# A four-layer gated transformer on one core: in layer 0, GpSimd makes the squares, cubes and sums of the spline bases in halves

## What is computed

```
out = _layernorm(res + out, ln_g, ln_b)          # res is the query projection
base = silu(out) @ base_w.T
for k in range(1, SPLINE_ORDER + 1):             # SPLINE_ORDER is 3; eight bases remain
    bases = (x - grid[:, :-(k+1)]) / (...) * bases[..., :-1] + (grid[:, k+1:] - x) / (...) * bases[..., 1:]
spl = bases.reshape(rows, -1) @ (spline_w * spline_scaler[..., None]).reshape(D, -1).T
return base + spl
```

## Time and profile before

| | us |
|---|---|
| median of 3 runs | 2756.57 |
| lowest, highest run | 2755.38, 2758.04 |
| the profiled execution | 2756.28 |
| its span, first to last instruction | 2754.5 |
| busy: PE, PEld | 2611.9, 1980.6 |
| busy: DVE, ACT, POOL | 1544.9, 1297.4, 642.9 |
| L629, GpSimd's cubes, 32 of them | 70.0 |
| L638, its sums, 32 | 66.7 |
| L624, its squares, 32 | 56.0 |

### The profile page before, as it was taken

One profiled execution on the slowest core, in us unless ns is written; L12 is line 12 of the kernel. 1 busy time (PEld: TensorE's weight loads), 2 busy tenths in 40 slices (PEclk: granted clock), 3 DMA queues, 4 the chain that ended last, 5 costly groups with the idle time before them and its releaser, 6 DMA issues. The chain is left out here.

```text
span 2754.5 us, 56714 instructions
## 1 busy us (share of the span) xinstructions
PE 2611.9 (95%) x19818; PEld 1980.6 (72%) x19818; DVE 1544.9 (56%) x4177; ACT 1297.4 (47%) x3610; POOL 642.9 (23%) x626
## 2 busy tenths in 40 slices
PE   6999978999999999989899998999998999989998
PEld 4777755666666666656677766999996777768887
DVE  4777846555555555535787874332335888842222
ACT  4777733343434334331576663333335777732222
POOL 1666661000000000000444441222221111113232
PEclk9999989999999999989999999999999999999999
DMA  4000002000000000010000005999992000059896
GB/s 124 18 18 18 12 4 107 14 13 7 13 7 13 7 13 7 1 34 1 19 20 19 24 7 210 334 327 328 329 326 76 24 19 24 7 207 311 303 313 224
DMA packets 91812, 267.57 MB, mean 97 GB/s; under 512 B 25068, under 2 KB 50805, under 8 KB 77269
## 3 DMA queue, kind: packets, MB, share of 16 engines
q1 hardware_dynamic: 74356, 242.53, 25.4%
q0 software_dynamic: 13632, 18.62, 3.2%
q10 hardware_dynamic: 3616, 3.67, 0.4%
HBM read 248.13 MB, written 16.65 MB: 96 GB/s over the span
## 5 line engine op out<-in xcount | busy, mean ns | idle before, releaser
L825 PEld LDWEIGHTS a_full_ps<-ident,a_probs 112*125 112x125 f32 x2688 | 367.7, 190 | 118.4 <-issue 57.9
L1928 PEld LDWEIGHTS m_banks<-m_x_inT,m_w 128*128 128x128 f32 x3824 | 435.1, 192 | 15.2 <-issue 13.5
L1928 PE MATMUL m_banks<-m_x_inT,m_w 128*128 128x128 f32 x3824 | 442.2, 276 | 1.4 <-ACT m_x_inT L1999 0.9
L936 ACT ACTIVATE a_probs<-a_masked,a_negmax 112x375 f32<-112x375 f32 x512 | 305.8, 599 | 283.2 <-DVE a_negmax L1155 283.1
L825 PE MATMUL a_full_ps<-ident,a_probs 112*125 112x112 f32 x2688 | 414.1, 280 | 14.3 <-DVE a_pT L1181 5.2
L1181 DVE COPY a_pT<-a_full_ps 125x448 f32<-125x448 f32 x448 | 276.6, 621 | 230.0 <-PE a_full_ps L825 226.7
L725 PE MATMUL a_full_ps<-attention_room 128*125 128x256 f32 (+1 forms) x960 | 330.1, 473 | 9.7 <-ACT a_qT L926 3.9
L717 PE MATMUL a_full_ps<-attention_room 128*128 128x375 f32 x896 | 323.0, 489 | 13.8 <-PEq L1771 8.6
L1155 DVE CUSTOM_DVE_ANT_0 a_masked<-a_sc_ps,a_mask_add 112x375 f32<-112x375 f32 x512 | 249.8, 545 | 28.5 <-PE a_sc_ps L812 27.6
L936 ACT ACTIVATE a_probs<-a_sc_ps,a_negmax 112x375 f32<-112x375 f32 x384 | 216.7, 575 | 89.6 <-DVE a_negmax L1161 89.5
L843 PEld LDWEIGHTS a_o_ps<-a_pT,a_v 125*32 125x32 f32 (+1 forms) x5376 | 164.7, 118 | 128.7 <-issue 100.3
(11 more groups left out here) (253 smaller groups left out, 3480.7 us busy)
## 6 DMA issues: line engine op xcount, KB each, us to landing
m_w<-in_L2f_w SPq DMA_DIRECT2D x105, 1024.0 KB, 6.5
m_w<-in_L3f_w SPq DMA_DIRECT2D x72, 768.0 KB, 6.1
attention_room<-in_ctxT SPq DMA_DIRECT2D x64, 375.0 KB, 3.1
m_w<-in_L3f_w SPq DMA_DIRECT2D x36, 640.0 KB
m_b<-in_L2f_b SPq DMA_DIRECT2D x35, 128.0 KB, 8.2
p_rows<-normed SPq DMA_DIRECT2D x16, 224.0 KB, 6.3
attention_room<-in_L0x_spline_wT SPq DMA_DIRECT2D x1, 2048.0 KB, 10.6
net_room<-in_L1f_w SPq DMA_DIRECT2D x2, 1024.0 KB
```

The lines of the kernel that those rows point to most:

```text
L825: mm = pe.transpose(full_ps[0:KT, bank_of["turn", i, k], (j % 4) * S:(j % 4 + 1) * S], probs[:, i % 2, a, t * KT:(t + 1) * KT], ident[0:S, ...
L936: act.activation(probs[:, i % 2, a, 0:SK], src, ACT.Exp, bias=negmax[:, m:m + 1], scale=-1.0 if mask else 1.0, accum_out=rowsum[:, par, n: ...
L1928: mm = pe.matmul(ab_ps[:, (par * FC + f) % RING, i * SLOTS:(i + 1) * SLOTS], w[:, par, c, f * P:(f + 1) * P], x_inT[:, c, :], start=(c == ...
```

## The change

Each of GpSimd's squares, cubes and sums becomes two instructions, one for bases 0 to 3 and one for bases 4 to 7, of 448 numbers in a partition each. Both halves raise the semaphore, so a batch has 12 counts in place of 6, and every wait is set to the count of the second half. Results and the order of everything else are the same. The lines behind the change move down by up to 8: `square` is L627, `cube` L634, `add_bases` L645 in the changed kernel.

```diff
@@ -258,7 +258,9 @@
 KAN_SILU, KAN_CUBE1, KAN_LATE = 2, (0, 1), 3
 KAN_TANH, KAN_ABS, KAN_ACTS_EARLY = 0, (1, 2), 3
 KAN_NEAR2, KAN_NEAR1, KAN_SQ1, KAN_ACTS_LATE = (0, 1), (2, 4), (3, 5), 6
-KAN_SQ2, KAN_CUBE2, KAN_BASES, KAN_POOLS = (0, 2), (1, 3), (4, 5), 6
+KAN_SQ2, KAN_CUBE2, KAN_BASES, KAN_POOLS = (1, 5), (3, 7), (9, 11), 12
+
+BASE_HALVES = (slice(0, 4), slice(4, 8))
 
 
 def attention_stage(core, layer, heads, hd, scale, rope=False, mask=None, kan=False, moe=None):
@@ -621,12 +623,16 @@
                 def square(b, c):
                     pool.wait_ge(s_ka2.sem, s_ka2.at(b, KAN_NEAR2[c]))
                     pool.sem_inc(s_tick[3].sem, 1)
-                    pool.tensor_tensor(sq2[:, c], near2[:, c], near2[:, c], ALU.mult).then_inc(s_kp.sem, 1)
+                    for h in BASE_HALVES:
+                        pool.tensor_tensor(sq2[:, c, h], near2[:, c, h], near2[:, c, h], ALU.mult)\
+                            .then_inc(s_kp.sem, 1)
 
                 def cube(b, c):
                     pool.wait_ge(s_kp.sem, s_kp.at(b, KAN_SQ2[c]))
                     pool.sem_inc(s_tick[3].sem, 1)
-                    pool.tensor_tensor(near2[:, c], sq2[:, c], near2[:, c], ALU.mult).then_inc(s_kp.sem, 1)
+                    for h in BASE_HALVES:
+                        pool.tensor_tensor(near2[:, c, h], sq2[:, c, h], near2[:, c, h], ALU.mult)\
+                            .then_inc(s_kp.sem, 1)
 
                 def add_bases(b, c):
                     pool.wait_ge(s_k2.sem, s_k2.at(b, KAN_CUBE1[c]))
@@ -635,7 +641,9 @@
 
                         pool.wait_ge(s_out.sem, s_out.at(b - 1))
                     pool.sem_inc(s_tick[3].sem, 1)
-                    pool.tensor_tensor(bases[:, c], near2[:, c], near1[:, c], ALU.add).then_inc(s_kp.sem, 1)
+                    for h in BASE_HALVES:
+                        pool.tensor_tensor(bases[:, c, h], near2[:, c, h], near1[:, c, h], ALU.add)\
+                            .then_inc(s_kp.sem, 1)
 
                 def kan_body(t, par):
                     if exists(t - 2):
```

## The result

| | before | changed |
|---|---|---|
| median of 8 runs each, us | 2756.31 | 2764.58 |
| lowest, highest | 2754.88, 2758.04 | 2763.24, 2767.97 |
| ratio, 95% interval | | 1.0031, 1.0022 to 1.0039 |
| span of the profiled execution | 2754.5 | 2766.1 |

The change costs 8.3 us. The forecast was 2758.2 and its range ended at 2763.1; the result lies outside it, on the side of rival C, and beyond C's own 2761.9.

The account below looks back on a forecast made before the run. TensorE's own stream was taken to set the layer-0 loop's middle turns, one batch's chain its end. Terms 1.7 - 0.5 - 0.3 + 0 + 0.7 = +1.6 us gave 2757.9, forecast as a 2758.2 median; range 2754.8 to 2763.1.

Parts of the forecast that it names:

- rival C: Middle turns: first half of the sum ends before the residual add stands in line, second goes first; 2761.9 us, chance 0.19.
- The step that failed: Middle turns: residual add waits some 0.15 us for the sum's first half, ending near 271.6, and goes ahead of the second.
- turn 2: Layer-0 loop, turn 2: residual add held for half an instruction or not at all, giving back 0.3 to 1.05; taken -0.5 us.
- turns 3 to 14: Twelve middle turns of the layer-0 loop: with no slack, 12 x 0.14 = 1.7 us slower.
- turn 15: Layer-0 loop, turn 15: normalized rows wait for half a sum, 1.1 us shorter, but TensorE waits only 0.28: -0.3 us.
- turn 16: Layer-0 loop, turn 16: one delay more and one less on VectorE, 0 us, within 0.5.
- turn 17: Last batch: nothing covers the chain of square, cube, square, cube, sum; five splits, +0.7 us (0 to 2.5).
- The price of a split: Each GpSimd split costs 0.14 us (bounds nothing to 0.51); halves 0.93 and 1.13; busy time rises 13 us.
- No slack on VectorE's path: Layer-0 loop, residual add to normalized rows: a VectorE delay of 0.35 us costs 0.35 us; slack taken as none.
- B: Rival: splits nearly free, residual add meets no sum in the middle turns, VectorE only gains; -1.0, so 2755.6 us, chance 0.14.
- D: Rival: dear splits of 0.51 us each, the sum ending 2.5 us later in middle turns; 2770 us, chance 0.05.
- E: Rival: the change does nothing to the path because the waits are for whole pairs; 2756.6 us, chance 0.12.

Follow-up runs that it names:

- the kernel with the root early: All halved as in the changed kernel, but the next stage's inverse root L188 goes ahead of the one that waits for VectorE; 2765.26 us against 2756.73 before.
- the quarters: Kernel before with only GpSimd's sums split, each into four instructions of two bases; 2767.34 us against 2756.73.
- the extra square without a wait: Kernel before, nothing halved, plus one unused GpSimd square of 448 numbers right behind the sum of chunk 1; 2774.14 us against 2756.73.
- the kernel with the late sums: Kernel before, nothing halved, with the next batch's inverse root ahead of both sums instead of between them; 2849.41 us against 2756.95.
- the pair with and without a met wait: Kernel before plus an unused square behind chunk 1's sum, waiting for chunk 0's long-done sum (ratio 1.0058) or for the sum just ahead (1.0001).

## Why the prediction was wrong, step by step

**The step that failed** is the place of the first sum against the residual add, in the middle turns: that the first half of the sum ends at 271.6, after the residual add has started at 271.34, so that the add "waits for the first half, some 0.15 us, and goes ahead of the second". In the changed kernel the first half was over before the add began, and it met the second half whole: 0.92 us, not 0.56.

I had both halves of chunk 1's cube behind VectorE's L1254. Set by the residual add (256.26 there, 249.65 before, so 6.61 us apart, and a turn of 21.69), the changed kernel's second cube starts at 266.65, VectorE's cube ends at 268.81 (forecast: 268.5), the sum starts at 269.76 and its first half ends near 270.89, 0.45 us before 271.34. Only the second half of the cube stood behind VectorE's, not both. The value of rival C was 270.9, with the words "a first half that ends 0.7 us before my value". That part of the case was foreseen and given a chance of 0.19.

The other half of the step, that a residual add which stands before the boundary goes in there, did not fail. Turn 2 of the changed kernel run again shows it:

```profile
73.90 2.41 POOL L645 TENSOR_TENSOR a_bases<-a_near 128x448 f32<-128x448 f32 x2
...
74.19 1.13 DVE L1223 TENSOR_TENSOR a_res<-a_res,a_qtok 112x256 f32<-112x256 f32 x1
```

A half alone takes 1.13 us, so the first ended near 75.03. The add, ready 0.84 us before that, ended at 75.32, 0.29 behind the first half; the pair ended only at 76.31, 0.19 us longer than an undisturbed one. It was the same in turn 2 of the kernel with the root early (the add 0.62 us at 74.79, the pair 2.40 us from 73.99) and in two turns of the quarters, where it stood before the end of the third (0.47 us at 120.76, the four quarters 2.70 us from 119.05, not 2.51; 0.41 us at 367.85). In no turn of these profiles did the residual add stand before a boundary between the parts of a sum and fail to get in. So the 0.15 us may have been right for a first half that ends at 271.6; the sum did not come then.

For the normalized rows it is otherwise. In the changed kernel they too came after the first half was over, but the extra square without a wait and the quarters show that they can be ready before a boundary and still sit out what follows.

Of the working itself: the ends 271.45 and 271.95 should be 271.43 and 271.99 by their terms, and the earlier trace rows do not show the VectorE operation that began 0.6 us after the square of 3.22 us (L1254, at 68.97 in that trace). Neither changes the sum. Of the signs that were set, a period moved by more than 0.3 us came true, at 0.64, and L1084 got longer instead of shorter.

**The terms**, in us. The second column is from the profile whose turn 2 was undisturbed (the changed kernel run again, span 2764.5); the first profile agrees from turn 3 to 16.

| term | forecast | measured |
|---|---|---|
| turn 2 | -0.5 | -0.7 |
| turns 3 to 14 | +1.7 | +7.7 |
| turn 15 | -0.3 | +0.3 |
| turn 16 | 0 | +1.0 |
| turn 17 | +0.7 | +1.1 |
| sum | +1.6 | +9.4 |

The span grew by 10.0 in that profile, the medians by 8.3 and 9.0.

*The price of a split* was right: 0.93 and 1.13 us for the halves, 2.22 for a pair against 2.08, 0.14 more. By the Trainium skill's rule on consecutive Pool instructions (GPSIMD Engine Reference, Instruction dispatch) the split might have been free; no run here shows more of an overlap than some 0.04 us. What GpSimd's busy time grew beyond 96 x 0.14 = 13 is time in which its instructions were held, as my last sentence warned: the cubes alone have 16.4, with 4.5 for their splits.

*No slack on VectorE's path* was right, and it is what turned 0.64 us of holding into 0.64 us of period.

*The middle turns*: the residual add 0.51 instead of 0.14. It ends 0.28 us behind the sum; that sum starts 0.41 later and is 0.14 longer; of the 0.55, 0.04 was free. The rows of `resn`: I had written that L1223 "waits for its first half instead of the whole, and its end stays at the end of the row maxima". It went with the end of the pair, +0.13. L1084 and L195: the first was not relieved but got longer (1.34 at 270.60, not 1.06), the second was. The products' cover of the second half held; nothing was added there.

*Turn 2*: in the profile of the changed kernel run again, its residual add took 1.13 and TensorE waited 0.76 us, against 1.56 and 1.05. Here the add went in between the halves, as this term had it:

```profile
80.42 0.38 PE L776 MATMUL a_full_ps<-ident,a_resn 112*128 112x112 f32 x2 [0.76 <-DVE a_resn L1231]
```

80.42 is 0.70 before 81.12. In the first profile, of the slowest of the eight runs, this point comes at 83.25, +2.1; there the granted clock was 0.50 from 70 to 76 us (1.00 in the kernel before), the lower of its two levels (1.2 GHz; the higher is 2.4). TensorE had stood 2.6 us for ScalarE until 70.18. It is not in the second profile and so not what the change must cost.

*Turns 15 and 16*, the timeline of the changed kernel:

```profile
370.84 2.24 DVE L1231 TENSOR_SCALAR a_resn<-a_res,a_mv,a_rstd 112x256 f32<-112x256 f32 x1
...
387.30 3.06 POOL L645 TENSOR_TENSOR a_bases<-a_near 128x448 f32<-128x448 f32 x2
...
387.47 1.90 DVE L1262 SCALAR_TENSOR_TENSOR a_near<-a_sq,a_near 128x896 f32<-128x896 f32 x1
...
389.29 1.31 DVE L1257 SCALAR_TENSOR_TENSOR a_silu<-a_bend,a_lnT 128x224 f32<-128x224 f32 x1
```

L1231 was to wait for half a sum. It took 2.24 us against 2.10, the whole pair with its 0.14. Turn 15 gained nothing and lost 0.3. In turn 16 VectorE's cube goes in between the two halves of the sum (387.47 to 389.37; the pair takes 3.06 us, 2.22 undisturbed), and the SiLU is then held by the second half, 1.31 for 0.39 us. The forecast had 0 there; the turn took 1.0 more.

*Turn 17*, the last batch, against the earlier trace rows:

```profile
410.92 8.91 PE L793 MATMUL a_full_ps<-attention_room,a_bases 128*112 128x256 f32 x32 [2.96 <-POOL a_bases L645]
```

From the transposes to the products it is 17.43 us (393.49 to 410.92), 0.5 more than before (382.34 to 399.29). The forecast was 0.7, and the longer wait in front of L793 is there (2.96, 2.77). In the other profile turn 17 took 1.1 more, with a wait of 2.14 us there, since the products with the SiLU came later. The term lies between the two.

**The rivals.** C was the mechanism: 0.45 and 0.1 a turn there, 0.51 and 0.13 here. The 2761.9 counted only the 0.45, and fell short of the median by 2.7 us: 12 x (0.64 - 0.45) = 2.3 of it lie in the middle turns, the rest in the ends of the loop, which it had at -0.1. B needed a residual add that meets no sum in the middle turns, and D splits of 0.51; both are out by the lines. E is out by the result itself (1.0022 to 1.0039) and by the sums in quarters: waits for whole pairs do not make the change neutral if the pair is longer and VectorE at its edge.

**Open.** What decides at a boundary without a gap. Let in were the residual add between parts of a sum (above), VectorE's cube between halves of a cube (252.65, 249.47, 249.95) and of a sum (387.47), L195 between halves of a square (250.21), and L1092 between a cube and a square (it ended at 271.94, the square had started at 271.74). Not let in were the rows of `resn`, but once (0.82 us at 391.58 with the sums in quarters), L1092 between the halves of a cube (270.60, though that half ended 0.09 later), and the SiLU with both sums behind the root. That SiLU has a twin: in the changed kernel it is ready 0.84 us after the root's start (259.30 against 258.46) and the sum follows 1.30 us after it (259.76), to the hundredth as in the kernel with the late sums (249.94, 249.10, 250.40). It takes 0.38 us there and 4.81 here. In the changed kernel that sum waits for VectorE's cube, which ends at 259.38; with the late sums the one behind the root has nothing to wait for. This fits the pair with and without a met wait, but the halves that let VectorE in had nothing to wait for either. Nor does the start of a row tell who came first: with the root early GpSimd's second half starts near 248.27 + 1.13 - 0.04 = 249.36, some 0.6 us before VectorE's cube (249.95), which still takes its 1.08 us. The cases differ in operation, in what VectorE did just before, and in how long they had stood; no run here separates these.

## What to carry to other kernels

Splitting an instruction of one engine does not by itself give another engine a place in between. First work out on which side of the new boundary the other engine's instruction starts: 0.45 us on the wrong side made this change a loss. Where it starts on the right side, this case has both outcomes, so do not count on the place. Look at where the ends of the two engines' instructions lie against each other. Where a VectorE instruction on the critical path ends as shortly after a GpSimd one as here (0.15 and 0.32 us), it has next to no slack left towards it, even if it shows its shortest length: here each tenth that was added to the GpSimd run was paid, turn by turn. If something has to be put behind such an instruction, a wait that leaves a real gap can make it free, as it did for the extra square.

## What the runs showed of the hardware

- A VectorE instruction that meets GpSimd's can be held by a whole run of its instructions: the SiLU 4.81 us for 0.39 over an inverse root and two sums; `resn` 1.31 for 0.42 over a sum's end and a square. The Trainium skill has it that the two engines share their SBUF interfaces (GPSIMD Engine Reference, Key points); the rows agree that they contend, and the numbers here are for how long.
- A gap of 0.18 us on GpSimd, from a wait on its own last instruction, let the rows of `resn` in (0.42, period 21.70); a wait that was already met did not (1.31, period 22.59).
- At a boundary without a gap both outcomes occur: the residual add went in between two halves of a sum (1.13 us at 74.19, the second half 0.19 us longer for it), VectorE's cube between two halves of a cube (1.08 at 252.65); `resn` sat out a square behind a sum (1.31) and the SiLU two sums (4.81).
- A held VectorE instruction ended the same time after GpSimd's in every kernel above: 0.28 or 0.29 us for the residual add, 0.15 for the normalized rows. So a held length says when GpSimd was done, and nothing of the work.
- The other way, a second half of a GpSimd cube ended 0.99 to 1.00 us after VectorE's cube whenever GpSimd came to it (pairs of 3.15 to 3.76 us).
